# An audio tower layer: two layer norms between attention and router in groups of two, two and three tiles instead of four and three

## The reference, cut to what matters

```python
h = tokens @ W.T + b                       # 64 x 14 tokens of 128
a = layernorm(h)                           # no gain
o = attention(a) @ Wo.T + bo + a           # 8 heads of 16, over the 14 tokens of one batch row
h = h + layernorm(o) * gamma + beta        # first norm of this case ("norm 1")
x3 = layernorm(h)                          # second norm, no gain ("norm 2")
# feed-forward on x3: router (conv of 3 taps, gelu, conv of 3 taps) picks 2 of 10 experts,
# experts 128 -> 512 -> 128 with elu, shared conv of 9 taps -> silu -> 128
z = x3 + experts(x3, gates) + shared(x3)
h = h + layernorm(z) * ln_g + ln_b
```

## Time and profile before

| | |
|---|---|
| median of three runs | 183.19 us (182.43 to 183.86) |
| the profiled execution | 182.18 us, span 180.4 us |
| PE busy | 160.3 us, 89% of the span |
| DVE busy | 114.0 us, 63% |
| POOL busy | 76.0 us, 42% |
| ACT busy | 71.3 us, 40% |
| chain that ended last, by engine | PE 72%, DVE 10%, DMA 7%, ACT 6% |

### The profile page before, as it was taken

The page is one execution under the profiler, slowest core; times in us unless marked ns, Lnnn a source line. Parts: engine busy times, 40 slices in busy tenths (PEclk is TensorE's granted clock), DMA queues, the critical chain, the costliest instruction groups (busy, mean ns, idle before and its releaser), DMA issues.

```text
span 180.4 us, 3092 instructions
## 1 busy us (share of the span) xinstructions
PE 160.3 (89%) x1072; PEld 141.4 (78%) x1072; DVE 114.0 (63%) x309; ACT 71.3 (40%) x182; POOL 76.0 (42%) x70
## 2 busy tenths in 40 slices
PE   7798899999999589999999999989999999979500
PEld 2687688999664159999999997879999999969300
DVE  0177999979946969269020220499999999840562
ACT  3123746210025168004040404278787787830050
POOL 1042879999404450003777400015464554542040
PEclk9999999999999999999999999999999999999995
DMA  6999991000000000000999999109999411112503
GB/s 161 311 403 362 207 43 0 0 4 0 0 2 0 0 4 2 0 0 10 251 360 412 410 330 259 40 4 258 313 303 315 157 33 45 35 43 55 164 0 102
DMA packets 18658, 24.33 MB, mean 135 GB/s; under 512 B 4951, under 2 KB 14050, under 8 KB 18643
## 3 DMA queue, kind: packets, MB, share of 16 engines
q1 hardware_dynamic: 15894, 20.55, 39.8%
q0 software_dynamic: 1184, 2.44, 3.8%
q10 hardware_dynamic: 1564, 1.15, 2.5%
HBM read 19.71 MB, written 4.43 MB: 134 GB/s over the span
## 4 chain that ended last, share of the span: by engine, by line
PE 72%; DVE 10%; DMA 7%; ACT 6%; issue 2%; POOL 1%; ACTq 1%; DVEq 0%; POOLq 0%
PE psum L557 12%; PE psum L663 11%; PE psum L653 10%; PE psum L632 7%; PE psum L626 7%; PE psum L625 7%; PE psum L489 4%; DMA brow_s<-brow 3%; DVE stats L912 3%; DMA xb<-ys_rows 2%; PE psum L483 2%; PE psum L582 2%; ACT x L805 2%; PE psum L644 1%; DVE mv L915 1%
## 5 line engine op out<-in xcount | busy, mean ns | idle before, releaser
L445 POOL DMA_INDIRECT ys_rows<-yb,xid x23 | 22.1, 963 | 30.9 <-ACT yb L877 30.9
L868 ACT ACTIVATE eb<-psum,wring 128x128 f32<-128x128 f32 x92 | 26.1, 372 | 11.5 <-PE psum L653 10.2
L663 PE MATMUL psum<-wring,tb 128*128 128x128 f32 x184 | 24.8, 277 | 2.2 <-ACT yb L877 1.3
L1139 DVE SCALAR_TENSOR_TENSOR tb<-psum,wring,eb 128x128 f32<-128x128 f32 x92 | 25.9, 344 | 0.8
L663 PEld LDWEIGHTS psum<-wring,tb 128*128 128x128 f32 x184 | 22.3, 191 | 2.7 <-DVE tb L1139 2.7
L653 PE MATMUL psum<-xTb,wring 128*128 128x128 f32 x184 | 24.2, 275 | 0.0
L625 PE MATMUL psum<-xh,wsh_h 128*128 128x448 f32 (+2 forms) x72 | 23.6, 338 | 0.0
L626 PE MATMUL psum<-xl,wsh_h 128*128 128x448 f32 (+2 forms) x72 | 23.3, 337 | 0.0
L437 POOL DMA_INDIRECT xs_rows<-xT_s,slot x14 | 13.8, 983 | 21.1 <-DVE xT_s L1096 17.2
L399 POOL TENSOR_TENSOR rstd<-veps,mhalf 128x3 f32<-128x3 f32 (+2 forms) x9 | 8.3, 920 | 33.5 <-DVE veps L918 33.2
L653 PEld LDWEIGHTS psum<-xTb,wring 128*128 128x128 f32 x184 | 22.4, 192 | 0.0
(11 more groups left out here) (147 smaller groups left out, 236.0 us busy)
## 6 DMA issues: line engine op xcount, KB each, us to landing
wring<-wexp SPq DMA_DIRECT2D x23, 514.0 KB, 5.3
raw<-wsh SPq DMA_DIRECT2D x3, 768.0 KB, 8.2
xs_rows<-zero_s SPq DMA_DIRECT2D x1, 1472.0 KB, 17.7
xT_s<-xT SPq DMA_DIRECT2D x2, 384.0 KB, 5.9
xb<-xs_rows SPq DMA_DIRECT2D x1, 585.0 KB, 5.8
xb<-xs_rows SPq DMA_DIRECT2D x1, 520.0 KB, 5.3
rows_s<-rows SPq DMA_DIRECT2D x1, 384.0 KB, 5.6
ys_rows<-yb,xid POOLq DMA_INDIRECT x23, 2.6
```

The source lines that it names most:

```text
L445: pool.indirect_dma_start(ys_dram, bass.IndirectOffsetOnAxis(ap=xid[:, j:j + 1], axis=0), yb[:, j % NY, :], None)\
L663: ins = mm(ps[Y_BANK][:, 0:D], tb[:, j % NTT, c, :], wring[:, j % NR, W2 + c * P:W2 + (c + 1) * P], start=(c == 0), stop=(c == HC - 1))
L868: ins = A(eb[:, j % NEB, c, :], ps[U_BANKS[j % NU]][:, c * P:(c + 1) * P], ACT.Exp, bias=wring[:, j % NR, B1 + c:B1 + c + 1])
L1139: ins = V.scalar_tensor_tensor(tb[:, j % NTT, c, :], ps[U_BANKS[j % NU]][:, c * P:(c + 1) * P], wring[:, j % NR, B1 + c:B1 + c + 1], eb[:, ...
```

## The change

In norm 1 and norm 2 every engine now works in the three groups of norm 0 instead of two halves. POOL's `rstd`, DVE's statistics and `nmr`, gamma, the add and ACT's normalisation are done per group. ACT takes 1, 1 and 2 tiles of the groups' x3 and DVE 1, 1 and 1, so that each still does four and three. PE waits per group before the transposes, and tells of them per half as before. The list of DVE is also put in another order: `nmr` of group 0 of norm 1 comes before the statistics of group 2, that of group 1 behind them, that of group 2 behind the statistics of group 0 of norm 2. The last norm of the kernel keeps its two halves. The copies to `xh` and `xl` keep their two halves and their places.

```diff
--- before.py
+++ after.py
@@ -74,7 +74,7 @@
 V_BANK = (5, 7)
 XT_BANK = 3
 FILL = (11, 36, 6)
-ACT_TILES = 2
+X3_ACT = (1, 1, 2)
 
 HW = N // 2
 FHALVES = [(0, HW), (HW, N)]
@@ -251,11 +251,11 @@
         z_ps = bank_tiles((0, 1), TILES)
 
         def ln_tiles(n, k):
-            return TILES[k] if n else GROUPS[k]
+            return TILES[k] if n == 3 else GROUPS[k]
 
         def ln_count(n, k):
 
-            return len(GROUPS) + 2 * (n - 1) + k + 1 if n else k + 1
+            return n * len(GROUPS) + k + 1
 
         def tile_range(n, k):
             return slice(ln_tiles(n, k)[0], ln_tiles(n, k)[-1] + 1)
@@ -423,10 +423,10 @@
             pool.wait_ge(S("w_h_done"), 4)
             pool.tensor_tensor(wrc1_l[:], wrc1_s[:], wrc1_h[:], ALU.subtract).then_inc(S("rc_split"), 1)
             for n in (1, 2):
-                for k in range(2):
+                for k in range(len(GROUPS)):
                     inv_std(n, k)
-            pool.wait_ge(S("x3_act"), 2 * ACT_TILES)
-            pool.wait_ge(S("x3_dve"), NT - 2 * ACT_TILES)
+            pool.wait_ge(S("x3_act"), sum(X3_ACT))
+            pool.wait_ge(S("x3_dve"), NT - sum(X3_ACT))
             pool.tensor_tensor(h2[:], h2[:], rows_s[:, R_LNB:R_LNB + 1, :].broadcast_to([P, NT, D]), ALU.add).then_inc(S("h2_done"), 1)
             pool.wait_ge(S("xs_zero"), 32)
             pool.wait_ge(S("slot_done"), 1)
@@ -470,13 +470,16 @@
                     ins.then_inc(S("tok_mm"), 1)
 
             def transposes(src, done, banks, tag):
-                for hf in range(2):
-                    pe.wait_ge(S(done + "_act"), ACT_TILES * (hf + 1))
-                    pe.wait_ge(S(done + "_dve"), TILES[hf][-1] + 1 - ACT_TILES * (hf + 1))
-                    for i in TILES[hf]:
+
+                for g, tiles in enumerate(GROUPS):
+                    pe.wait_ge(S(done + "_act"), sum(X3_ACT[:g + 1]))
+                    pe.wait_ge(S(done + "_dve"), tiles[-1] + 1 - sum(X3_ACT[:g + 1]))
+                    for i in tiles:
+                        hf = 0 if i in TILES[0] else 1
                         col = (i - TILES[hf][0]) * P
                         ins = nc.tensor.transpose(ps[banks[hf]][:, col:col + P], src[:, i, :], ident_s[:])
-                    ins.then_inc(S(tag), 1)
+                    if g:
+                        ins.then_inc(S(tag), 1)
 
             def bias_row(n, o_ap, tiles, start):
 
@@ -798,10 +801,11 @@
             act.wait_ge(S("ld_cst"), 16 * 4)
             A(hcol[:], cols_s[:, C_SH1:C_SH1 + HC], ACT.Copy, scale=0.5).then_inc(S("hcol_done"), 1)
 
-            def normalise(n, dst, src, hf, tag):
-
-                act.wait_ge(S("nmr_done"), 2 * (n - 1) + hf + 1)
-                for i in TILES[hf][:None if n in (1, 3) else ACT_TILES]:
+            def normalise(n, dst, src, k, tag):
+
+                act.wait_ge(S("nmr_done"), (n - 1) * len(GROUPS) + k + 1)
+                tiles = ln_tiles(n, k)
+                for i in (tiles[:X3_ACT[k]] if n == 2 else tiles):
                     A(dst[i], src[i], ACT.Identity, bias=nmr[:, n, i:i + 1], scale=rstd[:, n, i:i + 1]).then_inc(S(tag), 1)
 
             def exps(hd):
@@ -824,10 +828,10 @@
                 act.wait_ge(S("cT_mm"), hf + 1)
                 A(cT[:, lo:hi], ps[2 + hf][:, 0:hi - lo], ACT.Copy).then_inc(S("cT_done"), 1)
 
-            for hf in range(2):
-                normalise(1, on_t, o_ps, hf, "on_done")
-            for hf in range(2):
-                normalise(2, x3_t, h2_t, hf, "x3_act")
+            for k in range(len(GROUPS)):
+                normalise(1, on_t, o_ps, k, "on_done")
+            for k in range(len(GROUPS)):
+                normalise(2, x3_t, h2_t, k, "x3_act")
             for hf, (lo, hi) in enumerate(HALVES):
                 act.wait_ge(S("x3T_mm"), hf + 1)
                 A(by_tile(xh[:])[:, TILE_RANGE[hf]], tile_columns(ps[2 + hf], hf), ACT.Copy).then_inc(S("xh_done"), 1)
@@ -920,13 +924,13 @@
             def ln_bias(n, hf):
 
                 dve.wait_ge(S("rstd_done"), ln_count(n, hf))
-                sl = TILE_RANGE[hf]
+                sl = tile_range(n, hf)
                 V.scalar_tensor_tensor(nmr[:, n, sl], mv[:, n, sl, 0], -1.0, rstd[:, n, sl], ALU.mult, ALU.mult)\
                     .then_inc(S("nmr_done"), 1)
 
             def normalise(n, dst, src, hf, tag):
 
-                for i in ln_tiles(n, hf)[ACT_TILES:]:
+                for i in ln_tiles(n, hf)[X3_ACT[hf]:]:
                     V.tensor_scalar(dst[i], src[i], mv[:, n, i, 0:1], rstd[:, n, i:i + 1], ALU.subtract, ALU.mult)\
                         .then_inc(S(tag), 1)
 
@@ -1022,21 +1026,25 @@
             for hd in (2, 3):
                 dve.wait_ge(S(f"o_sum{hd}"), 1)
                 context(hd)
-            for hf in range(2):
-                dve.wait_ge(S("o_mm"), hf + 1)
-                ln_stats(1, o_ps, hf)
-            for hf in range(2):
-                ln_bias(1, hf)
+            dve.wait_ge(S("o_mm"), 1)
+            for k in range(2):
+                ln_stats(1, o_ps, k)
+            ln_bias(1, 0)
+            dve.wait_ge(S("o_mm"), 2)
+            ln_stats(1, o_ps, 2)
+            ln_bias(1, 1)
             dve.wait_ge(S("hbeta_done"), 1)
-            for hf in range(2):
-                dve.wait_ge(S("on_done"), TILES[hf][-1] + 1)
-                sl = TILE_RANGE[hf]
-                link(V.tensor_tensor(on[:, sl, :], on[:, sl, :], bc(R_GAMMA).broadcast_to([P, len(TILES[hf]), D]), ALU.mult))
+            for k, tiles in enumerate(GROUPS):
+                if k == 1:
+                    ln_bias(1, 2)
+                dve.wait_ge(S("on_done"), tiles[-1] + 1)
+                sl = tile_range(1, k)
+                link(V.tensor_tensor(on[:, sl, :], on[:, sl, :], bc(R_GAMMA).broadcast_to([P, len(tiles), D]), ALU.mult))
                 link(V.tensor_tensor(h2[:, sl, :], on[:, sl, :], hbeta[:, sl, :], ALU.add))
-                ln_stats(2, h2_t, hf)
-            for hf in range(2):
-                ln_bias(2, hf)
-                normalise(2, x3_t, h2_t, hf, "x3_dve")
+                ln_stats(2, h2_t, k)
+            for k in range(len(GROUPS)):
+                ln_bias(2, k)
+                normalise(2, x3_t, h2_t, k, "x3_dve")
             for hf, (lo, hi) in enumerate(HALVES):
                 dve.wait_ge(S("xh_done"), hf + 1)
                 cols = TILE_RANGE[hf]
```

## The result

The changed kernel took 181.74 us in the median of 16 runs (180.76 to 184.13), the kernel before 182.99 us in 16 runs beside it (181.58 to 184.20). The ratio is 0.9928, with a 95% interval of 0.9901 to 0.9955: 1.3 us faster, between 0.8 and 1.8. The forecast was 0.6 us. Timed twice more against the kernel before, the same kernel gave 0.9932 [0.9899, 0.9965] and 0.9958 [0.9909, 1.0006]. The three weighted together by their intervals give about 0.993, or 1.2 us with 0.35 either way. These ratios leave out a kernel's runs that took over 1.5% more than its own fastest, which drops 10 of the changed kernel's 40 runs here and 5 of the 83 of the kernel before. Over all runs the means differ by 1.1, 1.0 and 0.3 us, together 0.85 us with 0.4 either way, and in the third timing the two medians are equal (182.75 and 182.76 us).

A forecast was written before the change was run, and what follows sets the result against it. The wait chain through both norms was taken as the bound, DVE's paired waits in norm 1 the prize: 0.43 + 0.71 - 1.76 = -0.62, rounded to -0.6, from 183.19 to 182.6 us; range 181.7 to 183.8.

The forecast's parts named there:

- Bound and place: First statistics of norm 1 to first convolution matmul: wholly on the path, some 13.8 us, any saving passed on whole.
- the two brackets of norm 1: DVE's waits in norm 1, 0.80 us for POOL's second rstd and 0.68 us for ACT's fourth tile, claimed removable.
- The prices: Split costs on DVE, priced start to start: 0.43 us added in norm 1, 0.71 in norm 2, against 1.76 removed.
- the layout: DVE's new instruction list, timed from 52.61: gamma of group 0 at 55.69, last `veps` at about 61.58.
- No wait left: DVE in norms 1 and 2: all 1.76 us of waiting go; first `nmr` waits only about 0.01 us.
- The tail costs nothing: Behind norm 2's last `veps`: about 0.8 us of DVE work lies hidden under the last rstd, costing nothing.
- POOL beside DVE: POOL's powers beside DVE's gamma and add in norm 2: DVE is charged nothing, despite the skill's exclusion rule.
- Rival 2: DVE's adds and tail stand still through POOL's powers: +2.0 us, 184.2 by profile, 185.2 by median; chance 4%.
- The clock: PE's gap ahead of the transposes gets shorter, about 1.3 us, so nothing speaks for a lower clock; charged nothing.
- Part 4: The tail, from norm 2's last `veps` through transposes, including PE's gap and clock: costed at nothing.
- theory B: Chain and clock, in the experiments: the longer old gap loses more clock, so the change saves part of that too.
- theory A: Chain alone, in the experiments: the change is worth its 0.55 us, the other half of the gain is chance.

The follow-up runs named there:

- a_again: The changed kernel timed again with no edit, beside the kernel before: 190.94 us median, ratio 0.9932 [0.9899, 0.9965].
- the cut ones: Old and changed kernels stopped behind the shared convolution's first pass, router's rest, experts and last norm left out: means over both sets 79.0 and 78.1 us.
- b_cut: The kernel before, cut off behind the first pass of the shared convolution over chunk 0, later parts left out: median 78.8 us.
- a_again2: The changed kernel timed a third time with no edit, against the kernel before: 182.75 us, ratio 0.9958 [0.9909, 1.0006].

## Why the prediction was half right

- **Bound and place.** Right. The stretch was on the path, the two brackets of norm 1 went, and what moved at the end of the norms reached the convolution.
- **The prices.** Right. Forecast -0.62 in all (the layout put the last `veps` at 61.58, -0.59); measured -0.55 at the last `veps` and -0.55 to -0.58 on the yardstick in each pair of profiles without a fall (74.15, 74.16 and 74.15 against 74.71, 74.71 and 74.73). The parts fit as well: from the first statistics to gamma the layout had 3.08 us and the profile 3.12, from there to the last `veps` both have 5.89. Start to start was the right measure: two tiles' statistics 0.53, gamma 0.45.
- **No wait left.** Right within 0.04 us: the first `nmr` waited for POOL that long (the power took 0.73 instead of 0.70).
- **The tail costs nothing.** Right. The last rstd and what follows it are as long as before: without a fall the convolution starts 13.18 us after the first statistics (a_again, 51.16 to 64.34), where the prediction had 13.2. And the three-way transposes brought nothing.
- **POOL beside DVE.** Right. The adds at 55.46, 57.33 and 59.25 met a running power and took 0.42, 0.42 and 0.56 on time; the powers stretched instead, 0.87 and 0.94 us where two columns alone took 0.70. Each of these powers also began while a gamma was running (55.01, 56.87, 58.66); that it was held up by that gamma is not ruled out by any run. Rival 2 did not happen. The rule of the Trainium skill ("SBUF — State Buffer", "Who interferes with whom"), by which the later of the two blocks fully, does not hold for these adds: not one of them waited.
- **The clock: the step that failed.** Part 4 put the clock at nothing: "nothing speaks for a lower clock" was read from one execution whose gap showed 1.00, a run without a fall. What the runs showed in its place: the clock falls in a part of the runs of both orders (8 of 12 and 6 of 12 of the cut ones). A fall puts the convolution off by 1.1 us in either order (after the first h, 58.28 us in b_cut against 57.19 in the kernel before, 57.73 in the first profile of the changed kernel against 56.63 in a_again). On the yardstick the changed kernel loses 1.45 us by it (75.60 against 74.15), so that it comes out 0.9 behind the kernel before without one. I carried a difference worked out at full clock over to a median that holds runs at both levels.

**What stays open** is what the recorded 1.2 us has beyond the chain. Shown: the chain's 0.56 us; that runs of both orders fall, at the same cost of 1.1 us up to the convolution; that with 24 filling matmuls nothing is left of the change (1.0008 and 0.9995). Not shown: that the changed kernel falls less often. 8 of 12 against 6 of 12 doesn't tell the orders apart (two runs in twelve would be 0.2 us in the mean), and the mean clocks of whole kernels pointed one way in one set and the other in the next. So that the clock makes the rest of the gain is theory B's claim and no result. Over all runs theory A is not excluded: the pairs with the gap filled (0.5, 1.0 and 0.8 us) give 0.8 together with 0.3 either way, the three timings with the gap 0.85 over all runs with 0.4 either way, and 0.56 lies in both. So the rest may be chance.

## What to carry to other kernels

Splitting a group is paid for where its engine is the one that everybody awaits, and earns only the waits that it closes; price both start to start; here the sum was right to a tenth of a microsecond. Before carrying that sum to a median, look at each run's mean clock: here the profiled run's 0.987 was that of the best quarter of the runs. For a gap on PE ahead of its densest work, ask for the granted clock in several executions; keeping the gap filled took 1 us off the cut kernels in either order, and off the means of the whole ones 0.2 and 0.7 us in the old order, 0.2 and 0.9 in the new one, each with 0.6 to 0.9 either way. And when a gain is near the scatter, set the means over all runs beside the ratio.

## What the runs showed of the hardware

The clock behind one and the same gap falls in some executions and not in others, with the same code: 1.00 throughout in a_again and 0.50 from 64.07 to 67.49 in a_again2, 74.15 and 75.62 us on the yardstick. The gaps ahead of these falls were 1.4 and 0.7 us in the changed kernel and 2.4 and 0.5 in b_cut.

In some sets of runs every kernel took 8 us more, also on a chip that ran the next set at the usual time (the kernel before: 191.6 and then 182.8 us median). The profiles place it in the shared convolution, while the experts' weights are loaded. Windows from a_again, one of these sets, and last the first of them in the kernel before:

```profile
90.00:100.00 10.00, 6.84 (x34) 5.48 (x32) 1.16 (x2) 1.91 (x2) 7.54 (x8) 0.97 0.99 363
100.00:105.00 5.00, 4.03 (x13) 3.53 (x13) 0.00 (x0) 0.00 (x0) 0.00 (x0) 0.50 0.73 191
...
90.00:100.00 10.00, 10.00 (x59) 9.46 (x57) 1.16 (x2) 1.91 (x2) 7.56 (x9) 1.00 1.00 385
```

In a_again PE idles for 3.2 us in the first window, with the DMA engines 99% busy, and for 1.0 us in the second, and waits for nothing that the profile names (the view of waits):

```profile
PE psum L628 <- issue: 2.7, 3, 1.0
PE psum L629 <- issue: 1.3, 2, 1.1
```

In the second window its clock is at half as well. Busy DMA engines alone are not the cause: in the kernel before they were as busy and PE had no gap. What the cause is, no run here shows.
